# Causal zeroing of the exponentials by VectorE, maxima in groups of eight and four, and the second norm's tokens by ScalarE

## The reference

```
h   = concat(patch_embedding(x), txt)                 # layer norm over 3840 taps, then a product with W
h   = h + attention(layernorm(h))                     # 12 heads of 16, causal, with a sink column, RoPE
h   = h + soft_moe(layernorm(h))                      # 64 slots, one expert (192 -> 768 -> 192) for each slot

attention: att = softmax([sink, where(causal, q k^T / 4, -inf)])[..., 1:];  y = (att v) Wproj * rezero
soft_moe:  xn = rms_norm(x) * norm_weight;  tok = xn / |xn|;  sl = slots / |slots| * scale
           logits = sl tok^T;  dispatch = softmax over tokens;  combine = softmax over slots
           y = dispatch xn;  y = expert(y);  out = combine y
```

## Time and profile before

| | us |
|---|---|
| three runs | 2916.89, 2918.97, 2924.98 (median 2918.97) |
| the profiled execution, its own time | 2921.78 |
| its span | 2920.0 |
| PE busy (matmuls) | 2694.3, 92% |
| VectorE busy | 1737.9, 60% |
| ScalarE busy | 1549.9, 53% |
| GpSimd busy | 950.7, 33% |
| granted TensorE clock, mean | 0.968 |

### The profile page before, as it was taken

One profiled execution on the slowest core, in us unless ns is written; L12 is line 12 of the kernel. 1 busy time (PEld: TensorE's weight loads), 2 busy tenths in 40 slices (PEclk: granted clock), 3 DMA queues, 4 the chain that ended last, 5 costly groups with the idle time before them and its releaser, 6 DMA issues. The chain is left out here.

```text
span 2920.0 us, 72392 instructions
## 1 busy us (share of the span) xinstructions
PE 2694.3 (92%) x25078; PEld 1976.1 (68%) x25078; DVE 1737.9 (60%) x7898; ACT 1549.9 (53%) x3185; POOL 950.7 (33%) x1814
## 2 busy tenths in 40 slices
PE   6799999999999999999999999999999998699955
PEld 5577777777777777777777777777777775355522
DVE  7466666666666666666666666666666665211133
ACT  2466666666666666666666666666666654111100
POOL 3333333333333333333333333333333332000000
PEclk8899999999999999999999999999999997699988
DMA  4333333333333333333333333333333321699988
GB/s 108 94 96 93 95 99 99 99 98 98 98 96 98 98 97 98 97 96 97 98 98 97 96 98 94 96 94 96 95 94 95 99 81 40 191 318 319 290 240 286
DMA packets 380043, 355.46 MB, mean 122 GB/s; under 512 B 37820, under 2 KB 345021, under 8 KB 379678
## 3 DMA queue, kind: packets, MB, share of 16 engines
q1 hardware_dynamic: 342310, 292.68, 36.1%
q10 hardware_dynamic: 37368, 58.15, 6.4%
HBM read 194.45 MB, written 40.30 MB: 80 GB/s over the span
## 5 line engine op out<-in xcount | busy, mean ns | idle before, releaser
L996 DVE CUSTOM_DVE_ANT_0 ps<-ps,late 128x325 f32<-128x325 f32 (+2 forms) x2304 | 748.5, 395 | 7.9 <-PE ps L474 4.0
L719 ACT ACTIVATE prob<-ps 128x590 f32<-128x590 f32 x768 | 500.8, 660 | 182.4 <-PE ps L497 168.0
L431 PE MATMUL ps<-window_w,xp 108*98 108x193 f32 x2304 | 497.4, 334 | 0.6 <-DVE window_w L953 0.6
L474 PE MATMUL ps<-kst,qst 99*128 99x325 bf16 (+2 forms) x2304 | 330.8, 253 | 38.3 <-DVE negmax L996 31.4
L431 PEld LDWEIGHTS ps<-window_w,xp 108*98 108x98 f32 x2304 | 335.8, 165 | 3.7 <-issue 1.5
L474 PEld LDWEIGHTS ps<-kst,qst 99*128 99x128 bf16 (+1 forms) x2304 | 199.7, 106 | 184.0 <-DVE negmax L996 136.7
L996 DVE DVE_READ_ACCUMULATOR2_ANT negmax<- 128x1 f32 (+1 forms) x2304 | 317.3, 138 | 0.0
L513 PE MATMUL ps<-prob,vaug 128*32 128x324 f32 (+2 forms) x4608 | 285.6, 340 | 0.0
L672 PE MATMUL ps<-xt,wqk 97*128 97x324 f32 (+1 forms) x768 | 251.9, 451 | 1.7 <-ACT xt L719 1.7
L491 PE MATMUL ps<-qst,kst 102*128 102x295 bf16 x768 | 228.8, 298 | 25.4 <-ACT prob L719 22.4
L1188 POOL TENSOR_TENSOR rot<-by 128x324 f32<-128x324 f32 x64 | 56.4, 881 | 599.4 <-DVE by L1095 599.4
(11 more groups left out here) (215 smaller groups left out, 5599.1 us busy)
## 6 DMA issues: line engine op xcount, KB each, us to landing
xw<-in_x_dram SPq DMA_DIRECT2D x384, 189.0 KB
qst<-part SPq DMA_DIRECT2D x768, 60.8 KB
w<-in_L_ffn_fc_weight_dram ACTq DMA_DIRECT2D x32, 1152.0 KB, 10.5
kst<-part SPq DMA_DIRECT2D x384, 81.0 KB
w<-in_L_ffn_fc_weight_dram SPq DMA_DIRECT2D x32, 768.0 KB, 8.7
h_held<-h_new SPq DMA_DIRECT2D x64, 288.0 KB, 3.7
kst<-part SPq DMA_DIRECT2D x768, 20.2 KB
w<-in_L_ffn_fc_weight_dram SPq DMA_DIRECT2D x64, 192.0 KB, 10.7
```

Of the source, the lines that this page charges most:

```text
L431: mm = pe.matmul(ps[0:TILE, BK7, half * (D + 1):(half + 1) * (D + 1)], xp[:, q, TILE * half:TILE * (half + 1)], window_w[:, q, :], start=( ...
L474: mm = pe.matmul(ps[0:nq, bk, col:col + keys], qst[i][0:MAX_ROW, h, q0:q0 + nq], kst[i][0:MAX_ROW, h, 0:keys], start=True, stop=True)
L719: return nc.scalar.activation(out_, in_, f, **kw)
L996: last = dve.tensor_tensor_reduce(out=ps[0:nq, bk, col:col + keys], in0=ps[0:nq, bk, col:col + keys], in1=late[0:nq, gone:gone + keys], sc ...
```

## The change

- `scores_t` loses the three products with `causal`: four matmuls a head are left, and the second key tile's columns now stand behind the third's. In their place VectorE takes, for two heads at a time, the minimum of the exponentials and a table `keep` that is 3e38 where the key counts and 0 where it is later. The values wait for that (`masked`) and not for the exponentials.
- The maxima are split in groups of heads 0 to 7 and 8 to 11 (before: 0 to 5 and 6 to 11). PE turns the first at head 10 (before: 8); the logits are turned at head 11 (before: 10).
- z becomes (h1 - mean) * alpha, by ScalarE (Identity with a scale and a bias) instead of VectorE. The norm's weight goes into the slots and into `kinds` once, in the preparation. For the sum of squares GpSimd forms z * weight (`zw`, in the buffer of `xhat`). beta is zss^-0.5 alone, and `disp` is a plain copy.

```
 def scores_t(b, i, h):
-    if h in (0, NH // 2):
-        max_in[h // (NH // 2)].wait(pe, b)
+    if h in (0, MAX_GROUPS[1][0]):
+        max_in[min(h, 1)].wait(pe, b)
...
-    pe.matmul(ps[:, bank, 0:EXPC], k0, q[:, 0:EXPC], start=True, stop=False)
-    pe.matmul(ps[:, bank, 0:127], causal[:], ident_b[:, 1:128], start=False, stop=True)
+    pe.matmul(ps[:, bank, 0:EXPC], k0, q[:, 0:EXPC], start=True, stop=True)
     pe.matmul(ps[:, bank + 1, 0:n0], k0, q[:, EXPC:T], start=True, stop=True)
-    pe.matmul(ps[:, bank + 1, c1:c2], k1, q[:, KTILES[1][2]:T], start=True, stop=False)
-    pe.matmul(ps[:, bank + 1, c1:c1 + 128], causal[:], ident_b[:], start=False, stop=True)
-    pe.matmul(ps[:, bank + 1, c2:EXPC], k2, q[:, KTILES[2][2]:T], start=True, stop=False)
-    pe.matmul(ps[:, bank + 1, c2:EXPC], causal[:], ident_b[:, 0:EXPC - c2], start=False, stop=True)
+    pe.matmul(ps[:, bank + 1, n0:c1], k2, q[:, KTILES[2][2]:T], start=True, stop=True)
+    pe.matmul(ps[:, bank + 1, c1:EXPC], k1, q[:, KTILES[1][2]:T], start=True, stop=True)
 def values(b, i, g, k):
-            exp_ready.wait(pe, b, 4 * g + 4)
+            masked.wait(pe, b, 2 * g + 2)

 # VectorE
+def mask(b, n):
+    exp_ready.wait(dve, b, 2 * n + 2)
+    heads = prob[:, 2 * n % 8:2 * n % 8 + 2]
+    for at, c0, nc_ in ((0, 0, FIRST), (FIRST, T, REST)):        # 127 and 197 columns
+        some = heads[:, :, c0:c0 + nc_]
+        last = dve.tensor_tensor(some, some, keep[:, at:at + nc_].unsqueeze(1).broadcast_to((128, 2, nc_)), ALU.min)
+    last.then_inc(masked.sem, 1)
 # its places in step:
   dmax; mt copy; lexp; +mask 0; dexp; +mask 1; stat; +mask 2; (rstd1) h_new, norm_stats; +mask 3;
   disp; +mask 4; (rstd2) xhat; +mask 5; y_all
-  z[t] = (h1[t] - mv2[t]) * nwb                                 # three scalar_tensor_tensor behind head 1

 # ScalarE, behind the copies of the values' projection
+  less_ready.wait(act, b - 1); ym_mm.wait(act, b - 2)
+  z[t] = Identity(h1[t], bias=less[t], scale=alpha[t])          # three
   zt copies
+  zw_ready.wait(act, b - 1, ...); squares of zw with sums       # moved from before the zt copies

 # GpSimd
   alpha as before
-  pw = alpha * alpha; (zs_ready) pw = zss * pw; max; power; beta_t = pw * alpha
+  less = -mean; less = less * alpha -> less_ready
+  (z_ready) zw[:, 2] = z[:, 2] * nwb; zw[:, 0:2] = z[:, 0:2] * nwb -> zw_ready
+  (zs_ready) beta_t = max(zss, 1e-10); power -> beta_ready

 # preparation: nw loaded earlier, three loads of nw as a column, kinds and slots multiplied by it,
 # keep made from the causal table turned by PE
```

More of the change, by code:

```diff
@@ L127, in early_fusion_kernel @@
                 z = tmp("z", [128, 3, D])
-                ynorm = xhat
+                ynorm = zw = xhat
                 xt = tmp("xt", [HALF + 1, 2, KEYS])
@@ L791, in step @@
                         if moe:
-                            act.drain()
-                            z_ready.wait(act, b - 1)
-                            beta_ready.wait(act, b - 2)
+                            less_ready.wait(act, b - 1)
+                            ym_mm.wait(act, b - 2)
                             for t, (_, nt) in enumerate(TTILES):
[L797 to L801, removed]
+                                last = fn(z[0:nt, t], h1[0:nt, t], ACT.Identity, bias=less[0:nt, t:t + 1],
+                                          scale=alpha[0:nt, t:t + 1])
+                            last.then_inc(z_ready.sem, 1)
                         if moe:
@@ L805, in step @@
                             fn(zt[:, 1], ps[0:HALF, BK4, 0:T], ACT.Copy).then_inc(zt_ready.sem, 1)
+                        if moe:
+                            beta_ready.wait(act, b - 2)
+                            for n, (t, (_, nt)) in enumerate(((2, TTILES[2]), (0, TTILES[0]), (1, TTILES[1]))):
+                                if n == 0:
+                                    zw_ready.wait(act, b - 1, 1)
+                                else:
+                                    act.drain()
+                                    zw_ready.wait(act, b - 1)
+                                last = fn(lexp[0:nt].rearrange("p t s -> p (t s)"), zw[0:nt, t, :], ACT.Square,
+                                          accum_out=zss[0:nt, t:t + 1])
+                            last.then_inc(zs_ready.sem, 1)
                         if front:
@@ L934, in prepare @@
                         dve.drain()
[L935 removed]
+                        dve.tensor_scalar(sl, sl, sn[:, 0:1], scl[:, 0:1], ALU.mult, ALU.mult)
+                        for c in range(2):
+                            dve.tensor_scalar(kinds[:, c], kinds[:, c], nw_col[:, c:c + 1], None, ALU.mult)
+                        dve.drain()
+                        dve.tensor_tensor(sl, sl, nwb[0:NS], ALU.mult).then_inc(slot_ready, 1)
                         dve.wait_ge(first_read, 1)
@@ L1000, in step @@
                                 last.then_inc(max_ready.sem, 1)
[L1001 to L1009, removed]
                             if moe and h == 9:
@@ L1033, in step @@
                             last.then_inc(c_ready.sem, 1)
+                        if att:
+                            mask(b, 0)
                         if moe:
@@ L1038, in step @@
                             dve.tensor_scalar(dexp[:], dexp[:], drec[:, 0:1], None, ALU.mult).then_inc(dn_ready.sem, 1)
+                        if att:
+                            mask(b, 1)
                         if front:
@@ L1047, in step @@
                                 ).then_inc(stat_ready.sem, 1)
+                        if att:
+                            mask(b, 2)
                         if front:
@@ L1058, in step @@
                             norm_stats(h_new[i], bn, mv1).then_inc(ln1_ready.sem, 1)
+                        if att:
+                            mask(b, 3)
                         if moe:
@@ L1061, in step @@
                             for n, t0, t1 in GROUPS:
-                                last = dve.tensor_tensor(disp[0:n, t0:t1], ps[0:n, BK4, NS * t0:NS * t1].rearrange(
-                                    "p (t s) -> p t s", s=NS), alpha[0:n, t0:t1].unsqueeze(2).broadcast_to(
-                                    (n, t1 - t0, NS)), ALU.mult)
+                                last = dve.tensor_copy(disp[0:n, t0:t1], ps[0:n, BK4, NS * t0:NS * t1].rearrange(
+                                    "p (t s) -> p t s", s=NS))
                             last.then_inc(dp_ready.sem, 1)
+                        if att:
+                            mask(b, 4)
                         if front:
@@ L1072, in step @@
                             last.then_inc(xhat_ready.sem, 1)
+                        if att:
+                            mask(b, 5)
                         if moe:
```

92 lines of the change are left out of this document (52 added, 40 removed).

## The result

The changed kernel takes 3225.86 us (median of 4 runs, 3216.44 to 3230.93) against 2921.97 for the kernel before on the same chip: a ratio of 1.1038, 95% interval 1.1006 to 1.1071, 304 us slower. The forecast was 3030 with a range of 2950 to 3085: slower was right, the size was wrong by a factor of 2.8.

The account below looks back on a forecast made before the run. VectorE paces the maxima, then PE and ScalarE alternate, and lateness at t = 27.27 lengthens all 64 steps. 1.85 us a step gives 118 us, plus 1 preparation: 3038 by the median, forecast 3030, range 2950 to 3085.

Parts of the forecast that it names:

- VectorE's price and order: Each mask: two VectorE operations, 0.83 us of queue, 0.91 to the end; the in-order queue makes PE's values wait.
- mask 3: VectorE's mask behind h_new's normalization, awaited by the values of heads 4 to 7: forecast from 25.9 to 26.8.
- The case without a lock: GpSimd's first operation not held by VectorE's mask: h_new at 23.2, +1.1 + 0.1 us a step, 2998; chance 0.25.
- From those values to 27.27: PE, from values of heads 4 to 7 to the products with the dispatch weights: 2.2 us, ending 29.05; +1.75 a step.
- The sum at full clock: 1.75 + 0.1 = 1.85 us a step, 118 us over 64 steps, plus 1 for preparation: 119 us.
- 29.05 less 27.27: Forecast against old time in the step of PE's products with the dispatch weights; given as +1.75 us.
- the first rival: No lock between VectorE's mask and GpSimd: +1.1 + 0.1 us a step, 2921.8 + 78 = 2998; chance 0.25.
- z: Second norm: VectorE's 1.07 us saved returns as its wait for PE; ScalarE's passes 0.9; worth 0 to 0.3, taken 0.
- The maxima: First group's DMA lands later, but dmax and dexp hold the first exponential anyway: cost 0 to 0.3 us, taken 0.1.
- The gain at head 6: Second maxima group needed only at head 8, removing PE's DMA wait at head 6: 0.64 us a step.
- The second rival: Faster: VectorE's idle time takes all masks, PE saves 1.4 to 2.0 us a step: 2813; chance 0.15.
- Identity: Rival: ScalarE's Identity not in the loaded table, two loads of 1283 ns a step, 164 us: about 3200; chance 0.02.

Follow-up runs that it names:

- e8: The changed kernel with VectorE's third mask moved behind the normalization of h_new, right in front of mask 3: 3255.31 us.
- e2: The changed kernel with idle identity products on PE, 5 before the mask wait at head 5 and 10 at head 9: 3057.83 us.
- e4: The kernel before with only the second norm's change, z made by ScalarE: 2969.95 us.
- e6: The changed kernel with VectorE's masks for heads 8 to 11 only, causal matmuls back for heads 0 to 7, z still by ScalarE: 2916.64 us.
- e5: The kernel before with VectorE's masks for heads 8 to 11 only and maxima in groups of eight and four; z stays with VectorE: 2902.88 us.
- e10: The kernel before with only the maxima in groups of eight and four: 2939.77 us.
- e1: The changed kernel without its six VectorE mask operations, so without the causal zeroing; values wait for the exponentials alone: 2846.8 us.
- e9: The kernel before with VectorE's masks for heads 8 to 11 only; maxima in groups of six, z by VectorE: 2888.82 us.
- e7: The changed kernel with mask 3 moved in front of VectorE's wait for rstd1 and h_new: 3153.35 us.

## Why the prediction was wrong

- **VectorE's price and order: right.** The masks' two operations take 412 and 560 ns (forecast 0.42 and 0.57), every start from mt to mask 3 is within 0.3 us in the step shown and within 0.5 in those beside it, PE's two gaps are 1.28 and 1.97 to 2.35 us by the matmuls (1.3 and 2), 0.2 more by the weight loads. The case without a lock is refuted by e8. That the price fits so closely is in part luck: the slope of 1.16 ns and the fixed 0.144 that the prediction reads from its rows give 0.44 and 0.60, and not the 0.42 and 0.57 that it goes on with.
- **The step that failed: "From those values to 27.27 it is 2.47 us now; two heads of 0.14 less, 2.2", and before it "a microsecond late at 27.27 is a microsecond of the period".** The durations were carried over from rows taken at 2.4 GHz into a step with a 2 us hole in PE's work. In the changed kernel this stretch took 3.36 us (1431.20 to 1434.56), in e2 at full clock 2.2, and what follows, which I had called untouched, ran partly at 1.2 GHz: the product L676 2.11 us against 1.26. e2 measures it: 2.6 us a step, 168 of the 304 us. No rival of mine had the clock in it. The trace of before carries a column for it that read 1.00, but PE's longest wait there, from 1000 to 2000 us, was 0.4 us.
- **The sum at full clock: 137 us measured (e2), 119 forecast.** The nearness is partly luck. The 137 hold up to 16 us of the idle products' own and about 14 us of z, neither of which was in the sum. Mask 3 ends 0.1 to 0.5 later than forecast. The two slips in the sums are small: 29.05 less 27.27 is 1.78 and not 1.75, and the first rival's 2921.8 + 78 is 3000 and not 2998.
- **z: nothing forecast, 49 us by itself (e4), 14 in company (e6 against e5).** The mis-sized term is ScalarE's three passes, 1.42 us instead of 0.9. The top of my bounds, 1.1, was also too low, because it was VectorE's own time and not a row of ScalarE.
- **The maxima: 0.1 us a step lost forecast, 0.34 lost by themselves (21 us, e10).** The first exponential, where the loss was looked for, is only 0.16 later in the changed kernel (16.54) and not late at all in e10; the loss stands in PE's order behind the late first head. The gain at head 6, kept for the second rival, does not exist.
- **The second rival's ceiling** (2813) is 34 us under e1; the 0.64 us that does not exist is 41 us of it.
- **Identity** caused no table load: ScalarE starts z 5 us into every step and nothing stands in front of it but GpSimd's product.

The parts measured alone (289, 49 and 21 us) add up to 359 and not 304. That z costs 14 us in company instead of 49 is 35 of the difference; where the other 20 go, no run shows.

## What to carry to other kernels

When a change opens a gap in TensorE's work, price what comes behind the gap at both clock levels; a trace in which the clock never fell tells nothing about it. Work for another engine is hidden only at its place in that engine's queue: six masks fitted into VectorE's idle time as a sum, and only the last two fitted where they stood, and those not in every step (e9). Before an idle row of PEld is counted as a gain, look whether PE is busy beneath it. And when a gap is filled with idle work to test for the clock, look in the trace whether the filling ends before the wait does.

## What the runs showed of the hardware

- A gap of 1.3 us and one of 2 to 2.4 us in TensorE's work, in each step of 41 to 44 us, brought the granted clock from 1.00 to 0.92 on the mean, with 3.4 to 10.2 us at the lower level behind the second. With the first filled it was 0.90, with the second filled 0.97, and three gaps of 1.3, 0.4 and 1.1 us gave 0.96 (e7). Five and ten idle products of 128 columns in the two gaps prevent it and pay 168 us, though they compute nothing. A gap of 1.1 us in each step with one or two of 0.4 to 0.5 behind it (z alone, e4) did not lower it.
- VectorE's operations with two SBUF inputs hold up GpSimd's small ones: 787 ns in the changed kernel against 196 in e8, and a power 1419 ns in e7 against 867 before.
- Three ScalarE passes of 98 to 128 partitions x 192 columns with a scale and a bias from SBUF take 1.42 us, VectorE's three with two tensors 1.07.
